# A new order of stages on every engine: key and head-output transposes next to the products of the retention

## The reference

```python
h = layernorm(x) * (1 + ca) + sa
q, k = rotary(h @ Wq.T), rotary(h @ Wk.T)          # 8 heads of 64
v, g = h @ Wv.T, h @ Wg.T                          # 8 heads of 128
scores = (q @ k.T) * D ** -0.5 * decay             # causal, gamma_h ** (t - s)
o = scores @ v
o = (o - mean(o)) * rsqrt(var(o) + EPS) * gn_weight + gn_bias
x = x + ga * ((o * silu(g)) @ Wo.T)
h = layernorm(x) * (1 + cb) + sb
xr, xk = mix of h and the token before it, by mu_r and mu_k
x = x + gb * (sigmoid(xr @ Wr.T) * (square(relu(xk @ Wk2.T)) @ Wv2.T))
```

## Time and profile before

| | |
|---|---|
| median of 3 runs | 790.91 us (789.59 to 791.45) |
| profiled execution, its own time | 789.19 us |
| its span in the trace | 787.4 us |
| TensorE, busy | 749.9 us, 95% |
| weight loads of TensorE, busy | 639.1 us, 81% |
| VectorE, busy | 600.4 us, 76% |
| GpSimd, busy | 587.7 us, 75% |
| ScalarE, busy | 434.1 us, 55% |
| granted TensorE clock, mean | 0.99 |

### The profile page before, as it was taken

One profiled execution on the slowest core, in us unless ns is written; L12 is line 12 of the kernel. 1 busy time (PEld: TensorE's weight loads), 2 busy tenths in 40 slices (PEclk: granted clock), 3 DMA queues, 4 the chain that ended last, 5 costly groups with the idle time before them and its releaser, 6 DMA issues.

```text
span 787.4 us, 28959 instructions
## 1 busy us (share of the span) xinstructions
PE 749.9 (95%) x12104; PEld 639.1 (81%) x12104; DVE 600.4 (76%) x1291; ACT 434.1 (55%) x798; POOL 587.7 (75%) x663
## 2 busy tenths in 40 slices
PE   4788999999999999999999999999999999999993
PEld 3467888888888888888888888888888888888783
DVE  6898779777878878887897878788788877776522
ACT  3334555556465555646555564655556465546562
POOL 3677868787777877788687877778777886776672
PEclk9899999999999999999999999999999999999997
DMA  9122222112212221221222122122212211221100
GB/s 305 41 43 42 42 42 42 40 26 55 42 35 58 42 67 26 68 42 37 56 42 66 27 68 42 33 59 42 66 26 70 42 35 44 42 55 36 24 14 27
DMA packets 63666, 39.60 MB, mean 50 GB/s; under 512 B 37936, under 2 KB 54448, under 8 KB 63408
## 3 DMA queue, kind: packets, MB, share of 16 engines
q1 hardware_dynamic: 62960, 36.92, 20.4%
q10 hardware_dynamic: 576, 0.83, 0.3%
HBM read 8.37 MB, written 4.19 MB: 16 GB/s over the span
## 4 chain that ended last, share of the span: by engine, by line
PE 88%; DVE 6%; issue 2%; POOL 2%; ACT 1%; DMA 1%; POOLq 0%; ACTq 0%; DVEq 0%
PE ring L243 48%; PE outs L243 15%; PE O_E L243 13%; PE ring L258 8%; PE O_O L243 2%; PE ring L282 2%; DVE turned L688 1%; DMA wmod<-in_w_mod 1%; POOL y L885 1%; DVE gn_sum L737 1%; DVE swapped L693 1%; DVE N L748 0%; POOL gn_rstd L878 0%; DVE qT L690 0%; POOL rot_k L868 0%
## 5 line engine op out<-in xcount | busy, mean ns | idle before, releaser
L885 POOL TENSOR_TENSOR y<-y,gate 128x512 f32<-128x512 f32 x128 | 163.3, 1294 | 51.0 <-ACT y L526 50.9
L243 PE MATMUL outs<-wo_gated,y 128*128 128x128 f32 x1024 | 141.6, 281 | 0.9 <-POOL y L885 0.7
L243 PEld LDWEIGHTS outs<-wo_gated,y 128*128 128x128 f32 x1024 | 126.7, 191 | 15.4 <-issue 10.6
L499 ACT ACTIVATE v_odd<-ring 128x512 f32<-128x512 f32 x64 | 38.4, 600 | 180.9 <-PE ring L243 165.1
L862 POOL TENSOR_TENSOR qT<-qT,swapped 128x512 f32<-128x512 f32 x64 | 81.7, 1277 | 51.8 <-DVE swapped L693 51.4
L737 DVE TENSOR_REDUCE gn_sum<-squares 128x4 f32<-128x512 f32 x128 | 81.9, 681 | 45.5 <-ACT squares L514 45.5
L878 POOL TENSOR_TENSOR gn_rstd<-gn_var,minus_half 128x8 f32<-128x8 f32 x64 | 105.4, 1647 | 5.1
L868 POOL TENSOR_TENSOR rot_k<-rot_k,sin_k 128x256 f32<-128x256 f32 x128 | 91.3, 736 | 8.5 <-DVE sin_k L710 8.5
L526 ACT ACTIVATE y<-ring,gn 128x512 f32<-128x512 f32 x128 | 92.6, 774 | 6.8 <-PE ring L258 5.7
L514 ACT ACTIVATE squares<-O_E 128x512 f32<-128x512 f32 x64 | 38.2, 597 | 81.1 <-PE O_O L243 81.1
L243 PEld LDWEIGHTS O_E<-v,A 64*64 64x64 f32 x1024 | 54.8, 132 | 30.7 <-issue 27.4
(11 more groups left out here) (110 smaller groups left out, 2058.3 us busy)
## 6 DMA issues: line engine op xcount, KB each, us to landing
v<-v_odd SPq DMA_DIRECT2D x128, 128.0 KB, 2.4
k_odd<-rot_k SPq DMA_DIRECT2D x128, 64.0 KB, 2.2
X<-in_x SPq DMA_DIRECT2D x16, 256.0 KB, 3.9
out<-X SPq DMA_DIRECT2D x16, 256.0 KB, 2.5
rotary_q<-in_const_q SPq DMA_DIRECT2D x1, 1024.0 KB, 8.8
N<-in_w_qkT SPq DMA_DIRECT2D x1, 512.0 KB, 5.1
N<-in_w_vT SPq DMA_DIRECT2D x1, 512.0 KB, 6.8
N<-in_w_gT SPq DMA_DIRECT2D x1, 512.0 KB, 9.6
```

The lines of the kernel that those rows point to most:

```text
L243: return e.matmul(o, lhsT, rhs, start=start, stop=stop, skip_group_check=True)
L885: e.tensor_tensor(y[:, n % NY, :], y[:, n % NY, :], gate[:, n % 2, :], ALU.mult).then_inc(sem["y"])
```

## The change

All functions stay as they are, and so does the work; only the order in which each engine calls them changes, and the step shifts with it. On TensorE `transpose_k(i)` now stands directly ahead of `attend(i - 1)`, `scores(i)`, `recall(i - 1)` and `state(i)`, and `turn_heads(i - 5)` directly behind them; before, both stood together between `project_out` and `project_k`. Both projections of v and both of the gate, `project_k`, `project_out` and the stages of the norms and the feed-forward part stand outside. `project_v` now makes v of block i in the step of `state(i)`, where it was one and two steps ahead. The gate projections and `turn_heads` come one step later against the products than before, so one more step runs ahead without them and one more behind. The other engines' orders are rewritten to go with it.

```diff
-        steps = range(-14, NCHUNK + 17)
+        steps = range(-30, NCHUNK + 11)
@@ tensor
-                for g in due(step - 12, GC, NGROUP):
+                for i in due(step, 1, NCHUNK):
+                    project_v(i, 0)
+                for i in due(step, 1, NCHUNK):
+                    project_v(i, 1)
+                for i in due(step - 5, 1, NCHUNK):
+                    project_gate(2 * i)
+                for g in due(step - 13, GC, NGROUP):
                     project_ffn_k(g)
+                for g in due(step - 11, GC, NGROUP):
+                    transpose_n(g, 1)
+                for i in due(step - 7, 1, NCHUNK):
+                    project_out(2 * i + 1)
...
+                for i in due(step - 5, 1, NCHUNK):
+                    project_gate(2 * i + 1)
+                for g in due(step + 4, GC, NGROUP):
+                    transpose_n(g, 0)
+                for i in due(step + 1, 1, NCHUNK):
+                    project_k(i)
...
+                for i in due(step, 1, NCHUNK):
+                    transpose_k(i)
                 for i in due(step - 1, 1, NCHUNK):
                     attend(i)
...
                     state(i)
+                for i in due(step - 5, 1, NCHUNK):
+                    turn_heads(i)
                 for i in due(step - 6, 1, NCHUNK):
-                    project_out(2 * i + 1)
+                    project_out(2 * i)
                 for m in due(step + 4, 1, NCHUNK):
                     project_q(m)
...
@@ scalar
+                for i in due(step - 5, 1, NCHUNK):
+                    gate_silu(2 * i + 1)
+                for i in due(step, 1, NCHUNK):
+                    copy_kT(i)
...
@@ vector
-                for g in due(step - 8, GC, NGROUP):
-                    residual(g)
-                for g in due(step - 10, GC, NGROUP):
-                    mix_shift(g)
...
@@ sync
-                for i in due(step - 4, 1, NCHUNK):
-                    swap_k(i)
...
-                for i in due(step - 3, 1, NCHUNK):
-                    swap_v(i)
+                for i in due(step + 21, 1, NCHUNK):
+                    swap_v(i)
...
+                for i in due(step + 21, 1, NCHUNK):
+                    swap_k(i)
```

More of the change, by code:

```diff
@@ L782, in _ @@
             for step in steps:
-                for m in due(step + 4, 1, NCHUNK):
+                for i in due(step, 1, NCHUNK):
+                    sum_squares(i, 0)
+                for i in due(step + 1, 1, NCHUNK):
+                    add_state(i)
+                for g in due(step - 10, GC, NGROUP):
+                    mix_shift(g)
+                for m in due(step + 5, 1, NCHUNK):
                     rotate_q(m)
-                for i in due(step - 1, 1, NCHUNK):
+                for b in due(step + 3, CB, B, 1):
+                    mod_input(b)
```

155 lines of the change are left out of this document (64 added, 91 removed).

## The result

The changed kernel is slower. Its median is 794.22 us (791.46 to 797.46, 19 runs) against 790.73 us (789.42 to 793.27, 19 runs) of the kernel before: ratio 1.0036, 95% interval 1.0023 to 1.0048, some 3 us. The forecast was 786.7 us, 4.2 us less than before; the time lies outside its range of 777 to 792.5 us, and on the other side. The profiled execution took 794.55 us, near the median; its span is 792.7 us, 5.3 us more than that of before. In the experiments each ratio is to runs of the kernel before taken beside them, whose medians lie between 790.99 and 791.83 us. One execution of all, of the kernel with the heads' transposes one place later, took 875.11 us at a mean granted clock of 0.844 and is in no ratio.

The account below looks back on a forecast made before the run. TensorE was taken to bound the kernel, busy 749.9 of 787.4 us and never waiting from 76 to 740 us. Terms −3.8 + 0 + 0.8 + 1.7 − 1.2 − 1.7 = −4.2 us gave 786.7 us; range 777 to 792.5 us.

Parts of the forecast that it names:

- The changes of kind: TensorE's switches between full-array work, half transposes and 64×64 products: fewer touch full work, cost falls 46.0 to 42.2 us, gain 3.8.
- R-to-T: TensorE's switch from 64×64 products (state) to half transposes (turn_heads): taken as 0.16 us, bounds 0 and 0.21.
- Rival A: The switch from 64×64 products to half transposes is free: 9.6 us more gained, 777.1 us; chance 0.13.
- The recorded sign: Steady steps between two attend starts: a plain step should take 10.45 us, against 10.50 before.
- The key's copy: ScalarE's copy of kT ahead of scores, now behind attend alone: hidden with 0.07 us to spare, cost 0.
- Rival B: The key copy ahead of scores is late: 0.15 us stall in each of 60 steps, 795.7 us; chance 0.12.
- Near misses, +0.8: Loops through VectorE and GpSimd, tight with mix_shift and bunched GpSimd work: 0.8 us in all, bounds 0 and 3.
- The DMAs of part 5, 0 us: swap_v and swap_k on SyncE's queue: keep taking turns, v lands in time for state; 0 us.
- The fill, +1.7 −1.2: Start of the kernel: one more loop-bound step costs 1.7 us; a VectorE wait for rot_k goes, −1.2 us.
- The drain, −1.7: End of the kernel: the wait for N shrinks by 1.2 us, the wait for y by 0.5 us.
- the moved 1.55 us: One turn_heads and one out projection more behind the last recall: work moved to the end, not added.
- The sum: All terms over the whole kernel: −3.8 + 0 + 0.8 + 1.7 − 1.2 − 1.7 = −4.2 us.

Follow-up runs that it names:

- the clean kernel: Changed kernel with the key's odd half copied ahead of the value's and five unused matmuls ahead of attend in steps 1 to 4: 790.01 us, ratio 0.9982.
- the key first: Changed kernel with the copy of the key's odd half (swap_k) ahead of the value's (swap_v) in SyncE's order again: 791.52 us, ratio 1.0009.
- the products: Changed kernel with five unused 512-column matmuls of weights directly ahead of attend in steps 1 to 4: 788.98 us, ratio 0.9979.
- products in 3 and 4: Changed kernel with five unused matmuls ahead of attend in steps 3 and 4 alone; with the key's odd half copied ahead of the value's: 790.45 us, ratio 0.9983.

## Why the prediction was wrong, point by point

- **The changes of kind: right, and in sum somewhat too low.** R-to-T, which no row of before had, is in the changed kernel 60 times: the last wave of `state` at 433.57, the transposes at 433.77, 0.20 us where 0.09 is usual, and these take 0.64 us instead of 0.60. That is 0.15 to 0.16 us, as taken. In order of time:

```profile
433.57 0.27 PE L243 MATMUL ring<-v,k_odd 64*64 64x128 f32 x1
433.77 0.71 PE L258 MATMUL ring<-consts,N 64*128 64x64 f32 x16
434.41 0.38 PE L243 MATMUL outs<-wo_gated,y 128*128 128x128 f32 x1
```

  Rival A is out, and the price of this pair agrees as well with the rule of the Trainium skill, "TensorEngine Tiling (Array Packing)", Key Properties, that changing the mode drains the engine. With the other causes removed forty steady steps gained 2.74 us where these prices give 2.0. The recorded sign, a plain step of 10.45 us, doesn't serve: the new order deals the stages of the norms and the feed-forward part out to the steps in another way, and its shortest steady step takes 10.86 us with TensorE never idle.
- **The key's copy: right.** No `scores` of the steady part waits for `kT`; the copy of the earlier trace rows now starts 0.50 us behind the transposes (441.93 against 441.43), as it did. Rival B did not occur. Only the first `scores`, in the fill, waited, 0.8 us.
- **Near misses, +0.8: too much for the clean kernel, where they cost 0.** The loops through `N` and `mix_shift` held. What came instead were the gaps at `state`, 2.2 us in the profiled execution, at a place that this part didn't look at.
- **The DMAs of part 5, 0 us: the first failed step.** I looked at the value's copy alone. The key's now stands behind it on SyncE's queue and behind the late copy of ScalarE: before, it had landed 5.0 to 8.3 us ahead of its `state` (in the nine steps from 429 to 521 us), now 0.1 to 2.7 us. So `state` waits for it in the profiled execution: 1.3 us once in the fill, and 1.0 us in the steady part, nearly all of it where a fetch of instructions makes the copy land in 3.4 us or more instead of 2.2. The other 1.2 us of its gaps are inside `state`, at block edges. Undoing that order brought 2.7 us between the medians (1.0036 to 1.0009 in the ratios, 2.1 us). The gaps ahead of `state` are gone in all four profiles with the key first, those inside it in three.
- **The fill, +1.7 −1.2: the second failed step, and the largest miss.** The 1.64 us of idle time ahead of `h_full` did go. As a count of work and waits the term was good: with the products in place the stretch from `attend(0)` to `attend(5)` is 2.3 us shorter than before, forecast 1.9, and with the key first alone `attend(0)` starts 0.2 us later than before, forecast 0.5. What was missing is a term for the clock. The profile of before showed that it falls at the start, 0.51 from 27.2 to 34.1 us; I treated idle time as free of price wherever it stood, and so its joining too. The profiled execution loses 4.3 us from `attend(0)` to `attend(5)` (49.04 against 44.74): 3.3 in the two steps in which the clock fell, 0.6 in the first step, with the wait for the key's odd half, and 0.4 in the fifth, with a gap inside `state` (84.16 us, number 194 modulo 256 too). Ahead of `attend(0)` it has 3.4 us more at half clock than before; other profiles of the new order have from 6.8 us, as before, to 17.1 us there, so this part is not the order's alone. In the medians, with the key first, the products bring 1.0009 to 0.9982, 2.1 us.
- **The drain, −1.7: the third failed step.** The waits of 1.53 and 0.70 us went as forecast, but two new ones took their place. In order of time in the changed kernel:

```profile
745.13 0.29 PE L243 MATMUL O_E<-v,A 64*64 64x128 f32 x1 [0.56 <-DVE N L748]
...
761.53 0.63 PE L282 MATMUL ring<-consts,normed 128*128 128x128 f32 x4 [0.71 <-ACT normed L485]
```

  The last `attend` has no key work ahead of it any more and meets the loop through `N`, and the last group's transposes come before its norm is ready. 2.2 us of waits became 1.3: −0.9 instead of −1.7. The whole stretch is 1.1 us longer even in the cleanest kernel, where the moved 1.55 us less 1.7 and 0.3 should have made it 0.5 shorter; some 0.8 us of that I can't name.
- **The sum.** In the cleanest profile the new order gains 1.4 us of span, and 0.9982 in the medians, where the forecast said 4.2 us. But 1.5 us of its start (+2.5) are the unused products ahead of `attend(0)`. The profile with the key first alone has none, starts as before (+0.2), has one fall in the fill, and gains 1.9 us of span. Its start with the cleanest kernel's other stretches would give 3.7 us, an estimate from two profiles that no run shows as a whole. The steady part is as forecast or better; the drain (+1.1 instead of −0.5) isn't. The changed kernel itself loses all of the gain to the clock, to waits for the key's late copy, and to the gaps inside `state`.

Open is why the edge of a block of instructions brings a gap inside `state` in some steps and not in others: the kernel with the key first has the same edges in `state` and no gap, with products in 3 and 4 added it has three. Open is also why the clock falls behind some idle pieces of 1.4 us and not behind others.

## What to carry to other kernels

Idle time that costs nothing where it is spread can cost time when an edit joins it (here 1.6 us for each step in which the clock fell): besides the sum of TensorE's idle time, look at its longest pieces where other engines set the pace, and keep some projections between the waits there. An edit that groups work by kind saves about the changes that it removes, 0.07 us a step here, which is small beside one bank, one queue or one copy that comes late; so read the margins of every transfer that the new order moves (landing to use), not only of the one that was late before. A copy that lands in 2.2 us as a rule and in 4.3 at worst needs a margin for the worst case. When two runs differ by a stretch of code that is the same in both, compare them at common points of the program before explaining the total.

## What the runs showed of the hardware that I had not expected

- The same kernel (key first) takes 787 to 796 us in single runs, in step with the mean granted clock of each (0.988 to 0.977), and the places of the falls in the fill differ between profiles of nearly the same kernel (59.6 and 69.9 us; 66.5 us; none).
- From the half transposes to 64×64 products TensorE pays 0.14 us, the other way 0.15 to 0.16 us. That is as much as from full-array work to either (0.14 us), and less than back to it (0.20 and 0.21 us).
- The copy of the key's odd half (two issues, 64 KB each) landed in 2.2 us as a rule, and in 3.2 to 4.3 us in 17 cases in which a 16 KB fetch of TensorE's instructions was in flight with it; ten more matmuls early in the program decide which copies are hit.
- TensorE can stand still for 0.1 to 0.7 us with nothing to wait for, always at the same place in a block of 256 of its instructions, 1.2 to 1.6 us behind the landing of a block.
